# Gathering the expert rows by an order made with one-hot products, in a gated-attention and mixture-of-experts layer

## The chip, the cores and the metric

The kernel runs on one core of one Trainium2 chip. The metric is the device time of that core in microseconds (us), the median of several executions. Work is spread by hand over five engines: TensorE (PE; its weight loads are shown apart as PEld), VectorE (DVE), ScalarE (ACT), GpSimd (POOL) and SyncE (SP, which here only issues DMAs). Each has its own instruction stream, and they meet at semaphores. All data is fp32; one fp32 matmul stands in the trace as two passes, each with its own weight load.

## The reference, cut to what matters

The input is 2048 tokens (2 batches of 1024) of width 256.

```python
h = layernorm(x) * (1 + ca) + sa
x = x + ga * gated_linear_attention(h)          # 16 heads, chunks of 64
h = layernorm(x) * (1 + cb) + sb                # "h2" in the kernel
probs = softmax(h @ gate_w.T)                   # 8 experts
top_p, top_i = top_k(probs, 2)                  # two experts a token
y = sum over the two experts e of top_p * ((silu(h @ fc1[e].T) * (h @ fc2[e].T)) @ proj[e].T)   # 176 wide
shared = (silu(h @ sfc1.T) * (h @ sfc2.T)) @ sproj.T                                             # 704 wide
x = x + gb * (y + sigmoid(h @ shared_gate.T) * shared)
```

## The kernel before, in words

Tokens go in 4 blocks of 512 (`BLK`), 16 tiles of 128. Attention is a software pipeline over the blocks, `s` = 0 to 4. In its last round and after it stand the parts of the shared expert. A part is either `U` (block, f): two halves SA and SB of the up projection for 128 hidden channels, `silu_up` on ACT and `mult_up` on DVE, six of them a block, the last one half as large; or `D` (block, jj): the down projection of two token tiles, evicted on DVE by `add_down`. `SHARED_PARTS` lists them in order, and `FILL_PLACES` says how many stand at each named place between the steps of the routing. The parts take turns in two PSUM banks, `work[0]` and `work[1]`, so each matmul of a part waits until the part before the last has been evicted. Parts of the last block from `EARLY_UP` on come after the experts.

Routing: the top two experts of each token are found on DVE; `picked` (one-hot rows) times a triangular matrix on PE gives each token's rank within its expert; `routing_b` turns ranks into `pos`, the place of the token's two copies in an order sorted by expert, in which each expert starts on a multiple of 128. There are at most 39 tiles (`ETILES`) of one expert each.

The sorted rows then go through HBM. SP fills `xs_sorted` with zeros (10 DMAs) while attention ends. POOL scatters the 16 token tiles twice, 32 indirect DMAs (line 592), each row with 7 columns behind its 256 values (token number, weight, batch and so on). When all have landed, SP loads the sorted rows by pairs of tiles (line 457) into `xt`, four pairs of room. POOL works out from the extra columns of a loaded pair where its results go (`goals`, lines 604 to 613).

Experts: for each pair, PE does `rows_T` (transposes), `up` (line 1710), `hid_T` and `down` (lines 1731 to 1738); ACT and DVE stand between; DVE's `evac_y` writes the weighted result to `yout`, two pairs of room, and POOL scatters it to its token's row of `ys_tokens` by `put_rows` (39 indirect DMAs, line 621). The groups 1 to 3 of eight tiles are one hardware loop (`Fori`) on PE, ACT, DVE and SP; POOL's instructions are written out.

Tail: when all results have landed, SP loads them back (8 DMAs, line 474). PE meanwhile computes the rest of the shared expert of block 3 (`U` from `EARLY_UP` on, then two `D`), DVE adds everything (`combine`, lines 1330 to 1336, and `add_scaled_down`, line 1043), and SP stores the output.

Of the kernel before, what the change touches and what calls it, by code (L numbers as in the profile page):

```python
# [23 lines left out]
P = 128  # L24
# [26 lines left out]
XS_ROWS = ESLOTS * P  # L51
HX = HID + 7
NOWHERE = 1 << 20
X_TOK, X_W0, X_BATCH, X_TURN, X_DW, X_NONE, X_EXP = range(HID, HX)
# [10 lines left out]
def unit_order():  # L65
# [58 lines left out]
    fill(NBLK, "scatter")  # L124
    for f in range(EARLY_UP, FTS):
# [9 lines left out]
EARLY_UP = 4  # L135
SHARED_PARTS += [("U", NBLK - 1, f) for f in range(EARLY_UP)]
FILL_PLACES = [(4, "gates", 1), (4, "half", 1), (4, "second", 1), (4, "norm", 5), (4, "stats", 1), (4, "ln", 3),
               (4, "transposed", 2), (4, "top2", 1), (4, "scatter", len(SHARED_PARTS))]
FILL = {}
for slot_, place_, n_ in FILL_PLACES:  # L140
    FILL[slot_, place_] = SHARED_PARTS[:n_]
    del SHARED_PARTS[:n_]
UNITS = unit_order()
# [10 lines left out]
def adaln_moe(nc, x, cT, wmod, wq, wk, wv, wg1, wg2, bg2, wgate, norm_w, wo,  # L154
              router, e_up, e_down, s_up, s_down, out):
    with ExitStack() as ctx:
# [9 lines left out]
        xs_dram = nc.dram_tensor("xs_sorted", (XS_ROWS, HX), F32, kind="Internal").ap()  # L166
# [12 lines left out]
        h2tok = sb("h2tok", [P, NTILE, HX])  # L179
# [17 lines left out]
        def part(n):  # L197
# [28 lines left out]
        zero_row = state[:, :, :, :, :].rearrange("p a g v c -> p (a g v c)")[:, 0:HX]  # L226
# [24 lines left out]
        wq_sb, wk_sb, wv_sb, wgate_sb, wo_sb = (sb(n, [P, KC, HID]) for n in  # L251
                                                ("wq_sb", "wk_sb", "wv_sb", "wgate_sb", "wo_sb"))
# [17 lines left out]
        iota_i = sb("iota_i", [P, ESLOTS], I32)  # L270
        iota_f = sb("iota_f", [P, ESLOTS])
# [24 lines left out]
        pos_u = sb("pos_u", [P, TOPK, NTILE], U32)  # L296
        texp = sb("texp", [P, ESLOTS])
        texp_u = sb("texp_u", [P, ESLOTS], U32)
        texp1 = sb("texp1", [P, ESLOTS])
        tok_i = sb("tok_i", [P, NTILE], I32)  # L300
        second = sb("second", [P, XPAIRS, 2])
        turned = sb("turned", [P, XPAIRS, 2, 3])
        goal = sb("goal", [P, XPAIRS, 2, 3])
# [4 lines left out]
        yout = er_pos[:, :, :].rearrange("p a (t c) -> p a t c", t=2)  # L308
# [6 lines left out]
        xs_zero = sem("xs_zero")  # L315
# [23 lines left out]
        picked_ready, rank_full, rank_read, dlog_ready, pexp_ready, posu_ready, texp_ready = (  # L339
            sem(n) for n in ("picked_ready", "rank_full", "rank_read", "dlog_ready", "pexp_ready", "posu_ready",  # L340
                             "texp_ready"))
        xs_ready, ld_xt, xt_full, xT_ready, up_full, esilu_done, h_ready = (
            sem("xs_ready"), [sem(f"ld_xt{i}") for i in range(XPAIRS)], sem("xt_full"), sem("xT_ready"),
# [56 lines left out]
        def _(sp):  # L400
# [60 lines left out]
            for q in range(XPAIRS):  # L461
                load_pair(q, q)
# [6 lines left out]
            for j, s in enumerate(ys_stored):  # L469
                sp.wait_ge(s, 16 * len(range(j, ETILES, 4)))  # L470
# [1358 lines left out]
```

## Time and profile before

| what | value |
|---|---|
| median of 3 runs | 430.16 us (429.12 to 430.85) |
| the profiled execution, its own time | 429.87 us |
| its span, first to last instruction | 428.1 us |
| mean granted TensorE clock in the span | 0.970 of full |
| instructions in the span | 9797 |

The span is 1.77 us shorter than the time of the same execution; what a change saves in the span it saves in the time. Of the span, roughly the first 240 us are attention and routing, up to 306 us shared parts while rows are scattered, up to 403 us the experts, and then the tail.

### The profile page before, as it was taken

To read this page: it belongs to the slowest core of one execution; us is meant where nothing else is said; L and a number is where in the kernel's file an instruction comes from. 1 tells how busy PE (TensorE), PEld (TensorE's weight loads), DVE (VectorE), ACT (ScalarE), POOL (GpSimd) and SP (SyncE) were. 2 spreads that over 40 slices of the span, in tenths; PEclk is the share of its full clock that TensorE was granted. 3 is DMA by queue.
4 is the path that set the end of the run, shared out by engine and by line. 5 is a ranking of instruction groups with operands and counts; after the bars stand their busy time and mean duration, and the time that the engine had idled before them with its cause. 6 is when DMAs were issued, how large, how long until landed. Compare 5 with 4: busy or idle time off the path is not lost.

```text
span 428.1 us, 9797 instructions
## 1 busy us (share of the span) xinstructions
PE 380.2 (89%) x3833; PEld 231.2 (54%) x3834; DVE 235.4 (55%) x543; ACT 143.6 (34%) x296; POOL 146.8 (34%) x252
## 2 busy tenths in 40 slices
PE   3988889999899998999989999519999999999795
PEld 3345656474656566447545546304566666666353
DVE  3169656896698579214824811014265555656457
ACT  3567337535561503430324011001334333332010
POOL 8405006100610440020000377744047667676400
PEclk9999999999999999999999999858999999999789
DMA  8930300000000000499900023240133333321098
GB/s 272 295 109 7 98 4 2 2 3 4 2 3 3 2 2 5 148 308 287 254 12 2 26 101 114 101 152 12 33 96 109 101 98 110 107 69 47 33 315 273
DMA packets 32573, 39.83 MB, mean 93 GB/s; under 512 B 4231, under 2 KB 29202, under 8 KB 32532
## 3 DMA queue, kind: packets, MB, share of 16 engines
q1 hardware_dynamic: 29124, 30.74, 24.8%
q0 software_dynamic: 3408, 8.51, 5.6%
q8 instruction: 29, 0.48, 0.5%
q14 instruction: 12, 0.10, 0.1%
HBM read 23.24 MB, written 16.91 MB: 94 GB/s over the span
## 4 chain that ended last, share of the span: by engine, by line
PE 73%; DVE 10%; another core or an unknown queue 6%; ACT 5%; issue 3%; DMA 1%; SPq 0%; DVEq 0%; ACTq 0%
PE work L1361 17%; PE at_ps L1710 12%; PE work L1394 5%; PE work L1375 4%; PE work L1731 4%; PE at_ps L1430 4%; PE work L1733 3%; PE work L1522 3%; PE work L1572 2%; PE at_ps L1394 2%; PE at_ps L1694 2%; PE o_even L1485 2%; PE work L1354 2%; PE at_ps L1572 1%
## 5 line engine op out<-in xcount | busy, mean ns | idle before, releaser
L621 POOL DMA_INDIRECT ys_tokens<-er_pos,goal_u x39 | 40.6, 1041 | 43.3 <-DVE er_pos L1285 37.5
L1710 PE MATMUL at_ps<-arena 128*128 x156 | 54.5, 472 | 0.4 <-ACT arena L847 0.4
L592 POOL DMA_INDIRECT xs_sorted<-h2tok,pos_u x32 | 31.7, 989 | 66.1 <-DVE pos_u L955 56.6
L1375 PE MATMUL work<-sdn_sb,hs 128*128 128x256 f32 x192 | 48.6, 395 | 5.9 <-issue 5.9
L641 ACT ACTIVATE hs<-work 128x512 f32<-128x512 f32 (+1 forms) x24 | 14.3, 596 | 112.0 <-PE work L1361 93.9
L1027 DVE TENSOR_TENSOR hs<-work,hs 128x512 f32<-128x512 f32 (+1 forms) x24 | 16.6, 691 | 58.1 <-PE work L1361 44.3
L1375 PEld LDWEIGHTS work<-sdn_sb,hs 128*128 128x128 f32 x192 | 34.3, 190 | 19.1 <-issue 15.9
L554 POOL TENSOR_TENSOR sq<-sq,sg 128x512 f32<-128x512 f32 x8 | 10.0, 1274 | 99.9 <-issue 99.9
L1361 PE MATMUL work<-h2T,sup_sb 128*128 128x512 f32 x80 | 36.1, 597 | 1.1 <-DVE hs L1027 0.7
L1710 PEld LDWEIGHTS at_ps<-arena 128*128 128x128 f32 x156 | 26.5, 190 | 14.9 <-issue 6.6
L851 ACT ACTIVATE arena<-at_ps 128x176 f32<-128x176 f32 x39 | 12.4, 318 | 57.7 <-PE at_ps L1710 43.0
L1361 PE MATMUL work<-hT,sup_sb 128*128 128x512 f32 x40 | 22.9, 741 | 9.4 <-DVE tmp L1057 8.8
L1285 DVE SCALAR_TENSOR_TENSOR er_pos<-work,goal,sq 128x256 f32<-128x256 f32 x39 | 17.2, 480 | 21.4 <-PE work L1738 20.5
L1361 PEld LDWEIGHTS work<-h2T,sup_sb 128*128 128x128 f32 x80 | 14.8, 190 | 19.0 <-issue 15.4
L1265 DVE TENSOR_TENSOR arena<-at_ps,arena 128x176 f32<-128x176 f32 x39 | 13.3, 342 | 20.4 <-ACT arena L851 17.9
L1126 DVE COPY_PREDICATED arena<-causal,at_ps 128x512 f32<-128x512 uint32 x32 | 20.5, 718 | 5.9 <-PE at_ps L1430 5.9
L1057 DVE SCALAR_TENSOR_TENSOR tmp<-work,sgate,rows 128x256 f32<-128x256 f32 x12 | 5.2, 478 | 32.6 <-remote 25.2
L1361 PEld LDWEIGHTS work<-hT,sup_sb 128*128 128x128 f32 x40 | 9.5, 243 | 23.3 <-issue 11.7
L1430 PE MATMUL at_ps<-arena 32*64 32x128 f32 x512 | 17.8, 278 | 3.3 <-DVE gate_pair L1106 1.9
L1430 PEld LDWEIGHTS at_ps<-arena 32*64 32x64 f32 x512 | 14.1, 131 | 9.6 <-issue 9.0
L1361 PE MATMUL work<-za,sup_sb 128*128 128x512 f32 x40 | 17.4, 595 | 0.6 <-DVE tmp L1057 0.6
L1522 PE MATMUL work<-wv_sb,hT 128*128 128x256 f32 x64 | 15.8, 387 | 2.1 <-ACT sg L782 1.7
(243 smaller groups left out, 750.5 us busy)
## 6 DMA issues: line engine op xcount, KB each, us to landing
xs_sorted<-state SPq DMA_DIRECT2D x10, 526.0 KB, 11.4
h2tok<-xs_sorted SPq DMA_DIRECT2D x20, 263.0 KB
arena<-ys_tokens SPq DMA_DIRECT2D x8, 512.0 KB, 7.4
arena<-in_e_up SPq DMA_DIRECT2D x8, 352.0 KB, 5.5
x_sb<-in_x SPq DMA_DIRECT2D x4, 512.0 KB, 6.8
out_rows<-x_sb SPq DMA_DIRECT2D x16, 128.0 KB, 4.0
sup_sb<-in_s_up SPq DMA_DIRECT2D x2, 640.0 KB, 4.9
hs<-in_wmod SPq DMA_DIRECT2D x1, 1024.0 KB, 7.4
```

The lines of the kernel that those rows point to most:

```text
L592: g.indirect_dma_start(out=xs_dram, out_offset=bass.IndirectOffsetOnAxis(ap=pos_u[:, k, t:t + 1], axis=0), in_=h2tok[:, t, :], in_offset=N ...
L621: g.indirect_dma_start(out=ys_dram, out_offset=bass.IndirectOffsetOnAxis(ap=goal_u[:, i:i + 1], axis=0), in_=yout[:, q % 2, u, :], in_offs ...
L1027: v.tensor_tensor(hs[0:m, f, :], linear, hs[0:m, f, :], ALU.mult).then_inc(hs_ready, 1)
L1126: v.copy_predicated(atm[:, n % 2, j, :], causal[:, :, :].bitcast(U32).rearrange("p r l -> p (r l)"), at_ps[j][:, :]).then_inc(atm_ready, 1)
L1285: v.scalar_tensor_tensor(out=yout[:, (u // 2) % 2, u % 2, :], in0=work[u % 2][:, 0:HID], scalar=goal[:, (u // 2) % XPAIRS, u % 2, 1:2], in ...
L1361: ins = t_.matmul(o[0:m, :], sup_sb[:, k, w, f0:f0 + m], h2T_of[blk][:, k, :], start=(k == 0), stop=(k == KC - 1))
L1375: ins = t_.matmul(o[:, t * HID:(t + 1) * HID], hs[0:m, f, tk], sdn_sb[0:m, f, :], start=(f == 0), stop=(f == FTS - 1))
L1394: ins = t_.matmul(o[:, :], w[:, k, gr * P:(gr + 1) * P], rhs[:, k, :], start=(k == 0), stop=(k == KC - 1))
L1430: ins = t_.matmul(at_ps[j][CHUNK * e:CHUNK * (e + 1), q * P:(q + 1) * P], kh[r, gr, c * CHUNK:(c + 1) * CHUNK], qeo[r, gr, c, :, :].rearra ...
L1522: ins = t_.matmul(o[:, t * HID:(t + 1) * HID], hT[:, k, tk], wv_sb[:, k, :], start=(k == 0), stop=(k == KC - 1))
L1710: ins = t_.matmul(at_ps[2 + u % 2][:, 0:2 * FE], xT[:, u % 2, k * P:(k + 1) * P], eup[:, bass.ds(e, 1), k, :].rearrange("p a n -> p (a n)" ...
L1731: t_.matmul(work[t][:, 0:HID], hTe[:, w % 2, t * P:(t + 1) * P], main[:, bass.ds(e[t], 1), :].rearrange("p a n -> p (a n)"), start=True, s ...
```

## The change

The sorted rows no longer go through HBM.

- Each block's h2 rows are stored to HBM as they are, in token order (4 DMAs by SP, `store_h2`). The zero fill, the 7 extra columns, the 32 scatters, SP's pair loads and POOL's `goals` go.
- `routing_b` splits `pos` into tile and row within the tile (four small DVE operations in place of one cast). `tile_columns` (DVE, three operations on 128x640 for each of the two copies) makes for each token the one-hot row of its tile, times its token number plus one, and times its weight. `row_columns` (DVE, two on 128x1024 for each copy) makes the one-hot row of its row. 32 products of the second with the first on PE (128 tokens each, 80 columns, summed in `at_ps[3]`) give the table `rec`: for every row and tile of the sorted order, the token and the weight. `read_records` (DVE) makes gather and scatter indices of it.
- POOL fetches the rows of each expert tile by an indirect DMA (39 gathers, `gather_pair`), four pairs first, then two more, and from then on two gathers after each pair's two scatters.
- `yout` has room for four pairs instead of two and stands in another buffer. DVE's groups 1 to 3 are written out instead of looped.
- `EARLY_UP` is 0 instead of 4: `U` (3,0) to (3,3) move from before the experts to behind them. Of the nine parts from `D` (1,1) to `D` (2,1), five stand at the place "places", before the 32 products, and four at "gather", behind them. In the tail the first three `combine` stand between the `mult_up`.

The core of the diff:

```diff
-EARLY_UP = 4
+EARLY_UP = 0
-               (4, "transposed", 2), (4, "top2", 1), (4, "scatter", len(SHARED_PARTS))]
+               (4, "transposed", 2), (4, "top2", 1), (4, "places", 5), (4, "gather", 4)]
@@ SP
+            def store_h2(b):
+                sp.wait_ge(h2tok_ready, b + 1)
+                sp.dma_start(h2_dram[b * BLK:(b + 1) * BLK, :].rearrange("(t p) c -> p t c", p=P),
+                             h2tok[:, b * TPB:(b + 1) * TPB, :]).then_inc(h2_stored, 16)
...
-            for i in range(ESLOTS // 4):
-                sp.dma_start(xs_dram[i * BLK:(i + 1) * BLK, :].rearrange("(t p) c -> p t c", p=P),
-                             zero_row.unsqueeze(1).broadcast_to([P, TPB, HX])).then_inc(xs_zero, 16)
-            sp.wait_ge(xs_ready, 16 * TOPK * NTILE)
-            for q in range(XPAIRS):
-                load_pair(q, q)
...
+            store_h2(NBLK - 1)
@@ POOL
-            for k in range(TOPK):
-                for t in range(NTILE):
-                    g.indirect_dma_start(out=xs_dram, out_offset=bass.IndirectOffsetOnAxis(ap=pos_u[:, k, t:t + 1], axis=0),
-                                         in_=h2tok[:, t, :], in_offset=None).then_inc(xs_ready, 16)
...
+            def gather_pair(q):
+                slot = q % XPAIRS
+                for u in range(min(2, ETILES - 2 * q)):
+                    i = 2 * q + u
+                    if q >= XPAIRS:
+                        pool.wait_ge(xt_full, i - EGRP + 1)
+                    g.indirect_dma_start(out=xt[:, slot, u, :], out_offset=None, in_=h2_dram[:, :],
+                                         in_offset=bass.IndirectOffsetOnAxis(ap=token_u[:, i:i + 1], axis=0)
+                                         ).then_inc(ld_xt[slot], 16)
...
-            for q in range(EPAIRS):
-                if q + 2 < EPAIRS:
-                    goals(q + 2)
-                put_rows(q)
+            pool.wait_ge(token_ready, 1)
+            for q in range(XPAIRS):
+                gather_pair(q)
+            pool.wait_ge(goal_ready, 1)
+            ahead = XPAIRS + 2
+            for q in range(XPAIRS, ahead):
+                gather_pair(q)
+            for q in range(EPAIRS):
+                put_rows(q)
+                if q + ahead < EPAIRS:
+                    gather_pair(q + ahead)
@@ DVE
+        def tile_columns(dve, v, steps, k):
...
+            steps.did(v.tensor_tensor(weight, iota_f[:, 0:ESLOTS].unsqueeze(1).broadcast_to([P, NTILE, ESLOTS]),
+                                      spread(tile_f[:, k, :]), ALU.is_equal))
+            steps.sync()
+            steps.did(v.tensor_tensor(token, weight, spread(tok_f[:, k, :]), ALU.mult))
+            steps.sync()
+            v.tensor_tensor(weight, weight, spread(pw[:, :, k]), ALU.mult).then_inc(rec_made, 1)
+
+        def row_columns(dve, v, k):
+            for t in range(0, NTILE, RCHUNK):
+                if k == 0 and t == 0:
+                    dve.wait_ge(h2_stored, 16 * NBLK)
+                v.tensor_tensor(in_row[:, k, t:t + RCHUNK, :], iota_f[:, :].unsqueeze(1).broadcast_to([P, RCHUNK, P]),
+                                row_f[:, k, t:t + RCHUNK].unsqueeze(2).broadcast_to([P, RCHUNK, P]), ALU.is_equal
+                                ).then_inc(rec_made, 1)
...
+            for n, (kind, blk, i) in enumerate(parts):
+                if n < 2:
+                    tile_columns(dve, v, steps, n)
+                (mult_up if kind == "U" else add_down)(blk, i)
+                if 1 <= n <= TOPK:
+                    row_columns(dve, v, n - 1)
+            read_records(dve, v, steps)
+            fill(NBLK, "gather")
...
-            with dve.Fori(1, ESLOTS // EGRP - 1) as grp:
+            for grp in range(1, ESLOTS // EGRP - 1):
                 group(grp * EGRP, grp * XPAIRS)
...
+            sums = iter(range(NTILE // 2))
             for f in range(EARLY_UP, FTS):
                 mult_up(NBLK - 1, f)
+                if f >= FTS // 2:
+                    combine(next(sums))
@@ PE
-            fill(NBLK, "scatter")
+            fill(NBLK, "places")
+            for k in range(TOPK):
+                for t in range(NTILE):
+                    if t % RCHUNK == 0:
+                        pe.wait_ge(rec_made, TOPK + k * (NTILE // RCHUNK) + t // RCHUNK + 1)
+                    ins = t_.matmul(at_ps[3][:, 0:NREC * ESLOTS], in_row[:, k, t, :],
+                                    in_tile[k][:, t, :, :].rearrange("p a i -> p (a i)"),
+                                    start=(k == 0 and t == 0), stop=(k == TOPK - 1 and t == NTILE - 1))
+            ins.then_inc(rec_full, 1)
+            fill(NBLK, "gather")
...
             pe.wait_ge(shev_done, 2 * NBLK - 2)
             pe.wait_ge(mln_done, 2 * NBLK)
             pe.wait_ge(rank_read, 2)
+            pe.wait_ge(rec_ready, 1)
```

## Rows read from the trace of the kernel before

**Rows 1.** The page: busy time, share of the span and instructions of each engine.
```profile
PE 380.2 (89%) x3833; PEld 231.2 (54%) x3834; DVE 235.4 (55%) x543; ACT 143.6 (34%) x296; POOL 146.8 (34%) x252
```
**Rows 2.** Chain that ended last, in order of time: start us, us, what.
```profile
241.70 17.43 PE work L1361 x40
...
261.55 25.82 another core or an unknown queue
...
288.31 16.33 PE work L1361 x32
```
**Rows 3.** Windows: busy us and instructions of each engine, clock, DMA.
```profile
262.00:288.00 26.00, 11.60 (x43) 7.45 (x41) 0.82 (x3) 0.00 (x0) 16.20 (x18) 0.77 0.34 116
...
306.00:398.00 92.00, 90.98 (x432) 59.62 (x431) 52.49 (x132) 32.60 (x95) 57.35 (x120) 1.00 0.30 90
```
**Rows 4.** Timeline 240 to 290 us: start, us, engine, line, operation, idle before.
```profile
240.78 0.87 DVE L1057 SCALAR_TENSOR_TENSOR tmp<-work,sgate,rows 128x256 f32<-128x256 f32 x2
...
241.80 1.66 POOL L592 DMA_INDIRECT xs_sorted<-h2tok,pos_u  x1 [56.60 <-DVE pos_u L955]
...
267.73 3.58 PE L1375 MATMUL work<-sdn_sb,hs 128*128 128x256 f32 x14
...
278.92 0.58 PE L1375 MATMUL work<-sdn_sb,hs 64*128 64x256 f32 x1 [0.81 <-issue]
...
284.68 48.69 SPq L457 DMA_DIRECT2D h2tok<-xs_sorted  x11
...
287.39 0.87 DVE L1057 SCALAR_TENSOR_TENSOR tmp<-work,sgate,rows 128x256 f32<-128x256 f32 x2 [25.18 <-remote]
```
**Rows 5.** DMA queues, 260 to 262 us: packets, MB, share of 16 engines.
```profile
q8 instruction: 1, 0.02, 3.2%
```
**Rows 6.** The page's groups: count, busy us, mean ns of one, idle before.
```profile
L621 POOL DMA_INDIRECT ys_tokens<-er_pos,goal_u x39 | 40.6, 1041 | 43.3 <-DVE er_pos L1285 37.5
...
L592 POOL DMA_INDIRECT xs_sorted<-h2tok,pos_u x32 | 31.7, 989 | 66.1 <-DVE pos_u L955 56.6
...
L1027 DVE TENSOR_TENSOR hs<-work,hs 128x512 f32<-128x512 f32 (+1 forms) x24 | 16.6, 691 | 58.1 <-PE work L1361 44.3
```
**Rows 7.** Chain in order of time: two `D` parts of block 0.
```profile
190.32 11.73 PE work L1375 x48
```
**Rows 8.** Timeline, smaller DVE operations and the rank products on PE.
```profile
234.66 0.49 PE L1683 MATMUL at_ps<-yT,tri 128*128 128x128 f32 x2
...
234.99 0.39 PE L1684 MATMUL at_ps<-yT,ones 128*128 128x128 f32 x2
...
235.48 0.29 DVE L919 COPY yT<-at_ps 128x128 f32<-128x128 f32 x1 [1.65 <-PE at_ps L1684]
...
236.67 0.17 DVE L929 TENSOR_SCALAR ntl_i<-cnt_i 128x8 int32<-128x8 int32 x1
```
**Rows 9.** Timeline from the start of the experts.
```profile
304.49 0.60 PE L1694 MATMUL at_ps<-ident,h2tok 128*128 128x128 f32 x4
...
313.15 1.45 PE L1710 MATMUL at_ps<-arena 128*128 x4
...
314.61 1.10 POOL L621 DMA_INDIRECT ys_tokens<-er_pos,goal_u  x1 [20.00 <-DVE er_pos L1285]
...
316.01 1.03 POOL L621 DMA_INDIRECT ys_tokens<-er_pos,goal_u  x1 [0.30 <-issue]
...
317.98 1.45 PE L1710 MATMUL at_ps<-arena 128*128 x4
```
**Rows 10.** Timeline of the tail.
```profile
403.23 6.60 PE L1361 MATMUL work<-hT,sup_sb 128*128 128x512 f32 x8 [0.63 <-DVE er_pos L1285]
...
406.19 7.17 SPq L474 DMA_DIRECT2D arena<-ys_tokens  x8
...
411.38 11.89 PE L1375 MATMUL work<-sdn_sb,hs 128*128 128x256 f32 x48
...
424.94 0.88 DVE L1043 SCALAR_TENSOR_TENSOR x_sb<-work,sgate,x_sb 128x256 f32<-128x256 f32 x2
```

More of the change, by code:

```diff
@@ L50 @@
 XPAIRS = EGRP // 2
-XS_ROWS = ESLOTS * P
-HX = HID + 7
 NOWHERE = 1 << 20
-X_TOK, X_W0, X_BATCH, X_TURN, X_DW, X_NONE, X_EXP = range(HID, HX)
+NREC = 2
+RCHUNK = 8
 NROUT = NE + 1
@@ L142 @@
     del SHARED_PARTS[:n_]
+assert not SHARED_PARTS
 UNITS = unit_order()
@@ L295, in adaln_moe @@
         pos = sb("pos", [P, TOPK, NTILE])
-        pos_u = sb("pos_u", [P, TOPK, NTILE], U32)
+        tile_i = sb("tile_i", [P, TOPK, NTILE], I32)
+        tile_f = sb("tile_f", [P, TOPK, NTILE])
+        row_f = sb("row_f", [P, TOPK, NTILE])
+        tok_f = sb("tok_f", [P, TOPK, NTILE])
         texp = sb("texp", [P, ESLOTS])
         texp_u = sb("texp_u", [P, ESLOTS], U32)
[L299 to L303, printed above, removed]
+        tok_i = sb("tok_i", [P, TOPK, NTILE], I32)
+        rec = sb("rec", [P, NREC, ESLOTS])
+        token_u = sb("token_u", [P, ESLOTS], U32)
+        turn_at, token_1, token_0, in_batch1, empty, goal = (yflat[:, i * ESLOTS:(i + 1) * ESLOTS] for i in range(6))
         goal_u = sb("goal_u", [P, ESLOTS], U32)
         row_step, row_gain = sq[:, 0, 0:HID], sq[:, 1, :].rearrange("p (a n) -> p a n", a=2)
-        yout = er_pos[:, :, :].rearrange("p a (t c) -> p a t c", t=2)
+        yout = h2T[:, :, :, :].rearrange("p a k (t c) -> p (a k) t c", t=2)
         ld_x = [sem(f"ld_x{i}") for i in range(NBLK)]
@@ L841, in _ @@
             fill(NBLK, "top2")
-            fill(NBLK, "scatter")
+            fill(NBLK, "places")
+            fill(NBLK, "gather")
             def evac_rows(i, u):
@@ L902, in routing_a @@
                             ALU.subtract).then_inc(dlog_ready, 1)
-            steps.did(v.tensor_scalar(h2tok[:, :, X_EXP], topf[:, 1, :], 1.0, None, ALU.add))
             dve.wait_ge(pexp_ready, 1)
@@ L1259, in _ @@
             fill(NBLK, "top2")
-            fill(NBLK, "scatter")
+            parts = FILL[NBLK, "places"]
+            for n, (kind, blk, i) in enumerate(parts):
[5 more added lines that the diff above has]
+            read_records(dve, v, steps)
+            fill(NBLK, "gather")
             def expert_h(i, u):
@@ L1284, in evac_y @@
                 dve.wait_ge(gain_ready, i0 + u + 2 - u % 2)
[L1285 to L1286 removed]
+                v.scalar_tensor_tensor(out=yout[:, u // 2, u % 2, :], in0=work[u % 2][:, 0:HID],
+                                       scalar=rec[:, 1, i0 + u:i0 + u + 1], in1=row_gain[:, u % 2, :],
                                        op0=ALU.mult, op1=ALU.mult).then_inc(y_out, 1)
             def y_slot_free(i0, u):
[L1291 to L1293 removed]
+                if i0:
+                    dve.wait_ge(ys_stored[u], 16 * (i0 // EGRP))
             def group(i0, q0, tiles=EGRP, first=False):
@@ L1684, in _ @@
             t_.matmul(at_ps[2][:, P:2 * P], ones[:, :], pv, start=True, stop=True).then_inc(rank_full, 1)
-            fill(NBLK, "scatter")
+            fill(NBLK, "places")
+            for k in range(TOPK):
[6 more added lines that the diff above has]
+            ins.then_inc(rec_full, 1)
+            fill(NBLK, "gather")
             def rows_T(i, u):
                 if u % 2 == 0:
-                    pe.wait_ge(ld_xt[u // 2], 16 * (i // EGRP + 1) if isinstance(i, int) else i0_loads(i, u))
+                    pe.wait_ge(ld_xt[u // 2], (32 if i + 1 < ETILES else 16) + 32 * (i // EGRP) if isinstance(i, int) else i0_loads(i, u))
                 at_least(pe, xT_ready, i, -1)
```

135 lines of the change are left out of this document (62 added, 73 removed).

## The prediction

> **What bounds the kernel now.** I read four views in this order. The page's first part says who is busiest: PE, 89% of the span, with DVE and POOL far behind [rows 1]. So a gain has to come out of PE's stream or out of the 11% in which it stands. The chain that ended last says where it stands: it is PE nearly everywhere, except for one piece of 25.82 us from 261.55 on that belongs to no engine [rows 2]. The windows put a size on it: from 262 to 288 us PE is busy 11.6 of 26 us, DVE 0.8, ACT 0, POOL 16.2, and the granted clock is 0.77; in the experts, 306 to 398, PE is busy 90.98 of 92 us [rows 3].
>
> The timeline shows what kind of gap it is [rows 4]. DVE waits for the first `D` of block 2 until 287.39 ("remote", so no instruction of the record explains it), though the matmuls recorded for it were over by about 267. PE's last recorded passes are sparse, up to 278.92, and then it waits for DVE. All this time POOL issues scatters, from 241.80 on; SP begins to load sorted rows at 284.68, and DVE goes on 2.7 us later. So PE's signals do not come through while POOL issues scatter behind scatter, and come back when that is over. A fetch on an instruction queue lies at the beginning of it [rows 5]; whether it is the cause no row says.
>
> What did the gap cost? PE's work from 241.70 to the experts is 40+4 passes of `U` of block 2 (17.43 + 1.73 = 19.2 us), two `D` (11.73 for 48 passes) and `U` (3,0) to (3,3), 32 passes at 17.43/40 = 0.436 us, 13.9 us [rows 2, 7]. That ends at 241.7 + 19.2 + 11.7 + 13.9 = 286.5; the experts begin at 304.49 [rows 9]. So 18 us are lost. Part of them was due anyway only if PE had been without work: the rows were in SBUF at about 287, the time the parts fill.
>
> **The change, part by part.**
>
> *Routing.* Four dependent operations of 0.17 us, 0.2 with their wait, take the place of one cast, and a few small ones go: +0.6 us before `D` (1,0) is evicted [rows 8], and PE waits for that eviction.
>
> *Columns on DVE.* A 128x512 operation takes 0.69 us [rows 6], a 128x128 one 0.29 [rows 8]: 1.04 ns a column. So 128x640 takes 0.82 and three with their waits 2.6 us; 128x1024 takes 1.22, two 2.4. `tile_columns` (0) stands before the eviction of `D` (1,1), whose bank the second half of `U` (2,0) needs: PE has the first half's 1.7 us as cover plus nothing else, so it stands about 2.4 us. `tile_columns` (1) delays `mult_up` (2,0), and PE stands another 0.5. The two `row_columns` fall beside matmuls (3.5 us a part against 2.4 + 0.69 on DVE) and cost nothing; were they not covered, 5 us. I take +3.0; bounds 1 (only what exceeds the bank turns) and 8.
>
> *32 products on PE.* 64 passes. The rank products, four passes with 128 columns and a new weight load each, start at 234.66 and 234.99, two passes in 0.33 including the first load, and both pairs are over in 0.72 us [rows 8]; the four transposes take 0.60 [rows 9]. Taking off the drain of the last (0.3), a pass is 0.11 us, and 80 columns cannot be under half of that. 64 x 0.11 = +7 us. Bounds: 3.5, and 0.165 a pass by the 0.33 for two, 10.6.
>
> *What follows.* `U` (2,4), (2,5) and two `D` as before. The zero fill, scatters and pair loads go with the 18 us of the gap. The 4 stores of h2 are long done: they are issued while DMA is idle or, the last, at about 220 us, 30 before `row_columns` waits for it. New is that nothing of PE's stands between the eviction of `D` (2,1) and the first `rows_T`: two evictions 0.87 [rows 4], crossings, and the load of the expert numbers into registers, for which there is no row uncovered. I take 3 us, between 1.2 and 4. POOL's gathers begin about 1.4 us after the products (five small DVE operations) and eight of them take 8 x 1.3 = 10.4, while the parts behind them take 5.2 + 11.7 = 16.9: covered, with 4 us to spare after landing.
>
> Start of the experts: 241.7 + 0.6 + 3.0 + 19.2 + 7 + 11.7 + 3 = 286.2 instead of 304.49, **-18.3 us**.
>
> *Experts.* PE goes through a pair in 317.98 - 313.15 = 4.83 us without a pause [rows 9, 3], and nothing of its work changes. POOL's does: per pair two scatters as now, two gathers in place of `goals`. The second scatter starts 1.40 us after the first, both together last 2.43 [rows 9]; the mean of one is 1.04 [rows 6] plus 0.30 between. At 1.34 each, four take 5.36, 0.53 more than PE. The lag grows over the 13 pairs that still have a gather behind them to 6.5 us. The gather of pair q + 6 is issued behind the scatters of q and needed three of PE's pairs later. From the first scatter at 1.5 us after PE's turn of a pair, 2.7 + 2.7 for the four DMAs and 2.4 to land leave 15.9 - 9.3 = 6.6 us. So it just holds. `yout` with four pairs tolerates more than that. Price per indirect DMA: 0.99 + 0.30 at the low end (lag 4.3, hidden) and 1.66 + 0.30 at the high end, the one on DVE's busy moment at 241.80 [rows 4], which would be 7.8 us a pair, (7.84 - 4.83) x 13 - 6.6 = 33 us. The 39 scatters of this very stage are the nearer row; I take **+0.5 us**. The written-out groups on DVE cost nothing: DVE has 40 us to spare here [rows 3].
>
> The Trainium skill, page SBUF — State Buffer, section "SBUF: two separate sides", says that GpSimd can't write descriptors while DVE is in a two-port mode, as fp32 copies within SBUF are, and gives 3.1 us in place of 0.62. By it the sum would be far on the slow side if DVE's work here were such copies. The scatters' 1.04 against 0.99 beside a nearly idle DVE says that it isn't.
>
> *Tail.* Four `U` parts more on PE at full clock, 13.9 us: PE's stream bounds the new tail, while result loads (7.17 us of issue from 406.19 on) and `combine` fit beside it [rows 10]. The eight passes at half speed (6.60 us) are there before and after. Now PE ends at 411.38 + 11.89 = 423.27, and DVE, kept by `combine`, gets to the last eviction at 424.94; three `combine` go ahead in the new order, so this 1.4 us goes. **+12.5 us**.
>
> Sum: -18.3 + 0.5 + 12.5 = -5.3 us; span 428.1 - 5.3 = 422.8, time 424.6. The profiled execution (429.87) is 0.3 below the median of the runs, so I say **424.7 us**.
>
> **The rivals.**
>
> *The gap comes back (slower).* The mechanism is that of [rows 4]: PE's signals are held while POOL issues DMA behind DMA. POOL will do so in the eight gathers, and through two thirds of the experts with pauses under 1 us. For it: nothing in the trace shows a cause that the change removes, other than the density. Against: in the experts scatters run by twos and PE isn't held. In the gathers it would cost at most 6 us, since PE's stream went on for some 5 us of matmuls after the last signal. In the experts a held PE soon leaves POOL without work, so one hold is about lag plus landing, 5 to 8 us; from one hold on it is no faster, with two it is 424.7 + 12 = 437. The skill's Runtime: NRT & Kernel Launch, section "Instruction fetch mechanics", has each engine fetch 16 KiB blocks by a DMA queue of its own, and calls it mostly hidden; [rows 5] fit the size, and the cost is not hidden if this is the cause.
>
> *POOL bounds the experts (slower from 1.55 us on).* At c us per DMA the delay is (4c - 4.83) x 13 - 6.6: 2 us at 1.37, 8 us at 1.5, 13 at 1.6. It speaks for it that each DMA now has a wait of its own: the pair's spacing is 1.40, not 1.30. 427 to 438 us.
>
> *Larger gain.* The clock stays full in the tail (-3.3 us: eight passes at 0.436) or covers are better: 418 to 421.
>
> *The shift does nothing.* If the gap were due work of PE and not a hold, the experts would start 18 us later than I say, and the time would be 443. The sparse passes and the late signal speak against it.
>
> **How the numbers follow.** The forecast (421 to 428) 0.60, larger gain 0.12, gap back 0.13, POOL-bound beyond 2 us 0.12, nothing gained from the gap 0.03. The range 419 to 433 leaves out about 0.2. Within 0.5% (428.0 to 432.3), about what a measurement of this kernel can tell from no change: half of the POOL case and a third of the gap's, 0.12; faster 0.72, slower 0.16.
>
> **What would show it.** First `rows_T` at 284 to 288 us; no piece of the chain over 5 us without an engine; the products 6 to 8 us with a spacing of 0.11; pairs at 4.83 us throughout, and POOL's lag behind the evictions growing by about 0.5 us a pair to the fourteenth; PE at the end of the chain, its last `D` some 14 us later after the experts than now. Wrong would make it: a piece "unknown queue" inside the experts, `rows_T` waiting for a gather, or products at over 0.2 us a pass.

## The result and the profile after

| | before | changed |
|---|---|---|
| median of 4 runs each, us | 430.5 (429.12 to 435.44) | 446.76 (441.86 to 447.23) |
| ratio | | 1.033, 95% interval 1.022 to 1.044 |
| profiled execution, us (span) | 429.87 (428.1) | 447.23 (445.5) |

The changed kernel is slower by 3.3% (here and below ratios compare the means of executions within 1.5% of the fastest of their kernel, while medians and ranges have all of them). The forecast of 424.7 us and its range up to 433 both missed; what came true of the mechanisms is told below. The page of the changed kernel, first the engines as in [rows 1], then the two groups of POOL and the eviction whose rows POOL scatters, as in [rows 6]:

```profile
PE 393.0 (88%) x3897; PEld 241.6 (54%) x3898; DVE 246.0 (55%) x561; ACT 143.3 (32%) x296; POOL 127.1 (29%) x154
...
L589 POOL DMA_INDIRECT h2tok<-h_rows,token_u x39 | 38.5, 987 | 105.2 <-DVE token_u L978 84.7
...
L598 POOL DMA_INDIRECT ys_tokens<-h2T,goal_u x39 | 40.6, 1040 | 40.0 <-DVE h2T L1321 30.4
...
L1321 DVE SCALAR_TENSOR_TENSOR h2T<-work,rec,sq 128x256 f32<-128x256 f32 x39 | 17.1, 480 | 43.4 <-remote 25.6
```

PE is busy 12.8 us longer than before. The 64 passes of the products are 7.1 of it; moving parts adds nothing; another 3.9 is that the experts' 156 up passes take longer (L1757, 500 ns each against 472 before). The last row says what the forecast doesn't have: DVE waits 25.6 us in the experts' evictions for something that the trace doesn't explain ("remote").

The chain in order of time (start, length, what) shows the whole head and then where the time went:

```profile
248.73 13.98 PE work L1399 x28
262.71 7.10 PE at_ps L1728 x64
269.81 3.48 PE work L1399 x8
273.29 1.72 PE work L1392 x4
275.01 11.73 PE work L1413 x48
286.74 1.98 issue
288.71 0.42 PE at_ps L1741 x2
...
307.52 4.60 another core or an unknown queue
...
323.90 3.23 issue
...
339.16 4.68 another core or an unknown queue
...
358.31 4.53 issue
...
365.26 3.61 another core or an unknown queue
...
376.29 4.00 another core or an unknown queue
...
409.68 19.09 PE work L1399 x40
```

The piece of 25.82 us of [rows 2] is gone: from 248.73 to 286.74 PE runs from part to product to part, and then stands 1.98 us. But six pieces of 3 to 5 us in which no engine of the chain works, four of them called "unknown queue" as the old gap was, stand inside the experts. The windows (us, then busy us and instructions of PE, PEld, DVE, ACT, POOL, clock, DMA share, GB/s) set beside [rows 3]:

```profile
262.00:288.00 26.00, 24.74 (x126) 17.96 (x124) 6.39 (x18) 1.19 (x2) 7.83 (x8) 1.00 0.14 41
...
306.00:398.00 92.00, 77.82 (x340) 49.36 (x339) 41.37 (x105) 24.79 (x74) 55.90 (x55) 0.94 0.24 75
```

PE went from 11.60 to 24.74 busy us in the first window, and from 90.98 to 77.82 in the second. One hold from near, in the timeline (start, us, engine, line, operation, idle before):

```profile
309.82 0.97 POOL L589 DMA_INDIRECT h2tok<-h_rows,token_u  x1 [0.30 <-issue]
...
312.15 0.88 DVE L1321 SCALAR_TENSOR_TENSOR h2T<-work,rec,sq 128x256 f32<-128x256 f32 x2 [4.32 <-remote]
312.21 0.32 ACT L836 ACTIVATE arena<-at_ps 128x176 f32<-128x176 f32 x1 [3.91 <-PE at_ps L1757]
...
313.44 1.02 POOL L598 DMA_INDIRECT ys_tokens<-h2T,goal_u  x1 [2.65 <-DVE h2T L1321]
...
313.98 0.69 PE L1778 MATMUL work<-arena 128*128 x2 [1.84 <-DVE arena L1307]
```

DVE waits for down products whose last pass is recorded as over by 308.8, ACT for up products of a later tile. Both are let go within 0.06 us of each other, 1.4 us after the end of POOL's last gather before its pause (309.82 + 0.97 = 310.79). POOL had paused for want of an eviction. Then everything resumes and PE, at last, waits 1.84 us for DVE. I call this a hold. The list of waits in the experts (289 to 409 us: engine, line, waited for, total us, times, longest) adds them up, and the windows behind it show the stretches of half clock in the experts:

```profile
DVE h2T L1321 <- remote: 25.6, 6, 4.8
...
PE work L1778 <- DVE arena L1307: 13.2, 7, 3.3
...
PE work L1778 <- issue: 3.2, 1, 3.2
...
ACT arena L836 <- remote: 13.1, 4, 5.7
```
```profile
327.70:331.10 3.40, 3.40 (x10) 1.61 (x9) 0.49 (x3) 0.61 (x2) 1.90 (x2) 0.50 0.33 107
358.40:361.80 3.40, 3.40 (x10) 1.77 (x9) 1.28 (x4) 0.01 (x1) 2.51 (x3) 0.50 0.26 88
385.70:389.10 3.40, 3.40 (x9) 2.30 (x10) 1.22 (x3) 0.70 (x2) 1.00 (x1) 0.51 0.19 41
```

DVE's six long waits are not one for one the chain's six pieces: the one from 351.25 to 356.06 lies beside work of PE's in the chain, and the piece at 358.31 is a wait of ACT's. What PE itself loses in these rows is 13.2 + 3.2 = 16.4 us of standing before the down products, less 2.3 that it also stands at the last two tiles before the change, and 3 x 1.7 us for three stretches at the lower clock (1.2 GHz), which begin 0.3 to 1.8 us after PE went on from a stand: 14.1 + 5.1 = 19.2 us.

**The account, stage by stage.** Start of the rank products, start and end of the experts, and the tail up to the end of the span, all in us:

| | rank products | experts | their length | tail |
|---|---|---|---|---|
| before | 234.7 | 304.5 to 402.6 | 98.1 | 25.5 |
| changed | 236.9 | 288.7 to 409.0 | 120.3 | 36.5 |

From the rank products to the experts it is 51.8 instead of 69.8: -18.0. The rank products themselves start 2.2 later, a drift of the stages in front, which the change hardly touches (over the profiled executions of all variants below it lies between 233.6 and 243.2). Experts +22.2, tail +11.0. Together 17.4 = 445.5 - 428.1.

### The profile page after: what moved, and what is told of

It reads as the page before. It is cut to its first block, busy times and chain, and to the rows that moved or that the text cites. A ratio compares the mean times of both kernels' runs of the same rounds, so it can differ in the third digit from the quotient of the medians.

```text
span 445.5 us, 9617 instructions
## 1 busy us (share of the span) xinstructions
PE 393.0 (88%) x3897; PEld 241.6 (54%) x3898; DVE 246.0 (55%) x561; ACT 143.3 (32%) x296; POOL 127.1 (29%) x154
## 4 chain that ended last, share of the span: by engine, by line
PE 71%; DVE 10%; issue 7%; ACT 5%; another core or an unknown queue 4%; DMA 1%; DVEq 0%; SPq 0%; ACTq 0%
PE work L1399 15%; PE work L1413 9%; PE at_ps L1757 8%; PE work L1432 5%; PE at_ps L1468 4%; PE work L1778 3%; PE work L1560 3%; PE work L1610 2%; PE work L1780 2%; PE at_ps L1432 2%; PE o_even L1523 2%; PE at_ps L1728 2%; PE work L1392 2%; DMA hs<-in_wmod 1%
## 5 line engine op out<-in xcount | busy, mean ns | idle before, releaser
L589 POOL DMA_INDIRECT h2tok<-h_rows,token_u x39 | 38.5, 987 | 105.2 <-DVE token_u L978 84.7
L1757 PE MATMUL at_ps<-arena 128*128 x156 | 58.4, 500 | 0.4 <-ACT arena L832 0.4
L598 POOL DMA_INDIRECT ys_tokens<-h2T,goal_u x39 | 40.6, 1040 | 40.0 <-DVE h2T L1321 30.4
L1321 DVE SCALAR_TENSOR_TENSOR h2T<-work,rec,sq 128x256 f32<-128x256 f32 x39 | 17.1, 480 | 43.4 <-remote 25.6
L1757 PEld LDWEIGHTS at_ps<-arena 128*128 128x128 f32 x156 | 28.4, 203 | 16.7 <-issue 9.3
L1778 PE MATMUL work<-arena 128*128 x40 | 12.9, 405 | 16.4 <-DVE arena L1307 13.2
L1302 DVE TENSOR_TENSOR arena<-at_ps,arena 128x176 f32<-128x176 f32 x39 | 13.2, 339 | 20.1 <-ACT arena L836 14.6
L1399 PE MATMUL work<-za,sup_sb 128*128 128x512 f32 x40 | 19.6, 645 | 3.4 <-DVE tmp L1086 3.4
L1399 PE MATMUL work<-hT,sup_sb 128*128 128x512 f32 x40 | 19.1, 639 | 0.6 <-DVE h2T L1321 0.6
L832 ACT ACTIVATE arena<-at_ps 128x256 f32<-128x256 f32 x39 | 14.8, 383 | 14.3 <-PE at_ps L1741 13.6
L1741 PEld LDWEIGHTS at_ps<-ident,h2tok 128*128 128x128 f32 x78 | 11.2, 145 | 12.7 <-issue 9.0
```

What stands on the lines that cost most here:

```text
L589: g.indirect_dma_start(out=xt[:, slot, u, :], out_offset=None, in_=h2_dram[:, :], in_offset=bass.IndirectOffsetOnAxis(ap=token_u[:, i:i + ...
L598: g.indirect_dma_start(out=ys_dram, out_offset=bass.IndirectOffsetOnAxis(ap=goal_u[:, i:i + 1], axis=0), in_=yout[:, q % XPAIRS, u, :], in ...
L832: a.activation(xT[:, u % 2, :], at_ps[u % 2][:, 0:KC * P], ACT.Copy).then_inc(xT_ready, 1)
L1321: v.scalar_tensor_tensor(out=yout[:, u // 2, u % 2, :], in0=work[u % 2][:, 0:HID], scalar=rec[:, 1, i0 + u:i0 + u + 1], in1=row_gain[:, u ...
L1399: ins = t_.matmul(o[0:m, :], sup_sb[:, k, w, f0:f0 + m], h2T_of[blk][:, k, :], start=(k == 0), stop=(k == KC - 1))
L1757: ins = t_.matmul(at_ps[2 + u % 2][:, 0:2 * FE], xT[:, u % 2, k * P:(k + 1) * P], eup[:, bass.ds(e, 1), k, :].rearrange("p a n -> p (a n)" ...
```

## The experiments

The disputed term is +22.2 us in the experts against the forecast's +0.5. The theories: (a) POOL's dense indirect DMAs hold PE's signals, as in the old gap; (b) the bytes they move do it; (c) POOL is simply too slow and PE waits for rows. The 18 kernels ran in five groups, each group on one chip (0, 4, 1, 6 and 15) with its own runs of the kernel before beside it; which chip the first measurement ran on isn't known.

**First group: fewer POOL operations, or lighter ones.** e1 leaves out all gathers behind the first eight, e2 lets SP store the results, e3 is the kernel before with two pauses in the scatters, e4 cuts the later gathers to a quarter of their rows.

```diff
@@ e1: only the first eight gathers
-            for q in range(XPAIRS, ahead):
-                gather_pair(q)
             for q in range(EPAIRS):
                 put_rows(q)
-                if q + ahead < EPAIRS:
-                    gather_pair(q + ahead)
...
-                if u % 2 == 0:
+                if u % 2 == 0 and isinstance(i, int) and i < EGRP:
@@ e2: SP stores, POOL's scatter is taken out
+            for i in range(ETILES):
+                r = i % (TOPK * NTILE)
+                sp.wait_ge(y_out, i + 1)
+                sp.dma_start(ys_dram[r * P:(r + 1) * P, :], yout[:, (i // 2) % XPAIRS, i % 2, :]).then_inc(...)
@@ e3: before, pauses in the scatters
+                    if k * NTILE + t in (13, 26):
+                        pool.wait_ge(hs_ready, 3 * FTS if k * NTILE + t == 13 else 3 * FTS + 3)
@@ e4: short gathers
-                    g.indirect_dma_start(out=xt[:, slot, u, :], ...
+                    m = P if q < ahead else 32
+                    g.indirect_dma_start(out=xt[0:m, slot, u, :], out_offset=None, in_=h2_dram[:, :],
+                                         in_offset=bass.IndirectOffsetOnAxis(ap=token_u[0:m, i:i + 1], axis=0)
```

> The changed kernel without its last 31 gathers: only the first eight tiles are fetched, the later tiles are computed from whatever rows stand in the buffer, so the output is wrong in those. POOL then has two scatters a pair in the experts, as in the kernel before. Theory (PE's signals are held while POOL issues DMA behind DMA without a pause): no hold, pairs at 4.83 us, the experts about 98 us instead of 120, time about 425. Rival (the written-out groups on DVE, or the new buffers, slow the experts): the experts stay near 120 us and the time near 447. Rival (gathered rows arrive late): also about 425, but then the second experiment tells.

> The changed kernel with the 39 result scatters replaced by 39 plain stores of the same bytes from SyncE's queue, in the order of tiles (the results land in the wrong tokens' rows). POOL has the 39 gathers alone; bytes, landings and completions are the same. Theory (it is the density of POOL's own DMA stream): no hold, experts about 98 us, time about 425. Rival (the volume of transfers or of completions, whoever issues them): holds stay, 440 to 447.

> The kernel before, with two pauses in its stream of 32 scatters: after 13 of them POOL waits until DVE has finished the last up part of block 2, after 26 until it has finished U (3,2). Nothing is left out. Theory: the long hold from 262 to 287 us breaks up, PE works on, the experts begin at about 295 instead of 304 us, time about 421. Rival (the gap is due to something at that place, not to POOL's stream): the gap stays, and the scatters end later: 430 to 437.

> The changed kernel with the gathers from the seventh pair on cut to 32 of the 128 rows, so that each moves a quarter of the bytes; the other rows are stale, the output is wrong in them. Same number of DMAs and completions. Theory (density of POOL's stream): a gather on 32 rows may take POOL less time, then pauses appear and holds shrink, between 425 and 440; if it takes as long (0.95 us), the holds stay, about 446. Rival (bytes moved): holds gone even if POOL's time per gather is the same, about 425.

Measured: the kernel before itself took 416.51 us here (415.1 to 418.34, 7 runs), 14 less than in the measurement above. e1 took 425.3, e2 426.86, e4 421.98 (one run each), e3 424.86 (ratio 1.0215, 1.017 to 1.026). The experts took 99.7, 98.2, 99.7 and 99.7 us in e1, e2, e3, e4. No hold in any of them; but since the changed kernel did not run here, that said nothing yet about the theories. e3 was the first real blow: with pauses it should have won by the gap, to about 421, and it lost 2% against its own kernel before. In it PE waits 9.47 us for the late rows:

```profile
296.40 1.11 PE L1696 MATMUL at_ps<-ident,h2tok 128*128 128x128 f32 x4 [9.47 <-DMA h2tok<-xs_sorted]
```

So on this chip there was no gap for the pauses to remove, and the scatters had no time to give away. e4 also settled less than was hoped: a gather of 32 rows costs POOL 0.92 us in the mean, nearly as much as one of 128, so only the bytes are fewer in it.

**Second group: both kernels again, and the moved parts.** e7 is the changed kernel with the four `U` parts back in front of the experts; e8 the kernel before with one `combine` between each two `mult_up` of the tail.

```diff
@@ e7
-EARLY_UP = 0
+EARLY_UP = 4
...
-               (4, "transposed", 2), (4, "top2", 1), (4, "places", 5), (4, "gather", 4)]
+               (4, "transposed", 2), (4, "top2", 1), (4, "places", 5), (4, "gather", 8)]
@@ e8: before
+            sums = iter(range(NTILE // 2))
             for f in range(EARLY_UP, FTS):
                 mult_up(NBLK - 1, f)
+                if f < FTS - 1:
+                    combine(next(sums))
```

> The changed kernel as it is, beside the kernel before, to see whether the holds are there in this place and time: in the first four experiments no hold of PE's signals was to be seen, and the kernel before took 416.5 us instead of 430. If the holds depend on the chip or the hour and not on the code: no hold, about 423 to 425, against 416 to 417 of before (ratio 1.015 to 1.02). If POOL's density alone made them: they come back with the 39 full gathers, experts near 120 us, 440 to 447.

> The kernel before as it is, for its profile beside the others of this call. If before is at 416 us again: no gap from 262 to 287 us, PE ends the shared parts at about 286.5, and the experts begin at about 289 instead of 304.5, where the rows' arrival (about 287) sets it. If it is at 430: the gap is there.

> The changed kernel with EARLY_UP at 4 again: U (3,0) to (3,3) stand before the experts, at the place behind the products, as in the kernel before. PE's stream is the same, only in another order. By the sum of the prediction the experts begin 13.9 us later and the tail is 12.5 us shorter, so +1.4, minus up to 2 us because PE now has work while the last down part is evicted: the same as the changed kernel within 2 us. Rival (the eight gathers or the results' way back are the bound somewhere): faster by more than 4 us.

> The kernel before with one combine moved between the two mult_up of the tail, the one part of the change's tail that it can take. DVE comes to the last eviction 1.4 us late now; one combine taken out of its way (1.4 us) gives at most -1.4 us, 0.3%. If the first results have not landed when DVE asks for them, mult_up (3,5) and so PE's down parts wait: up to +2 us.

Measured: before 432.51 (429.39 to 437.98, 13 runs), e6 432.6, e5 444.11 (ratio 1.028, 1.020 to 1.036), e7 443.47 (1.025, 1.017 to 1.032), e8 432.34 (0.9995, 0.995 to 1.004). This chip is of the kind of the first measurement, and may be the same one. e6 has the gap and e5 has the holds. The chain of e6 and the window of e5's experts:

```profile
265.91 25.77 another core or an unknown queue
```
```profile
306.00:398.00 92.00, 80.27 (x354) 51.09 (x352) 43.04 (x108) 26.44 (x77) 57.49 (x57) 0.94 0.24 74
```

e7 starts its experts 14.2 us later than e5 (302.1 against 287.9), has a tail of 25.3 instead of 37.9, and experts of 115.4 instead of 117.8. So 14 us of parts cost the same on either side of the experts, and the holds are there either way. e8 changes nothing that this measurement can tell; the -1.4 us that were the most to expect lie inside its interval. It has the gap too: DVE waits 25.17 us in it.

**Third group: does the changed kernel have holds where before has no gap?** e9, e10 and e11 are e1, e2 and e3 again, e12 the changed kernel.

> The kernel of the first experiment (last 31 gathers left out, wrong rows in the later tiles) again, since the holds were absent from all kernels of the first call and present in all of the second. Beside a before of 430 to 433 (a chip with holds): theory of POOL's density says no hold, experts about 98 us, 425 to 428, that is below before; if PE's signals are held whatever POOL does, 440. Beside a before of 416: 425 again, no news.

> The kernel of the second experiment (scatters replaced by SyncE's plain stores, results in wrong rows) again. On a chip with holds: if the cause is POOL's own stream of indirect DMAs, no hold, about 427; if it is the volume of transfers and completions whoever issues them, holds stay, 436 to 447. On a chip without: 427 again.

> The kernel before with two pauses in its scatters, again. On a chip with holds: the hold lasts as long as POOL's stream does, so the first pause ends it or it does not begin before the last six scatters; the experts begin at about 296 instead of 304, and the time is 420 to 425 against 430 to 433. If the gap does not depend on pauses: 436 or more. On a chip without holds: 425 against 416.5, as in the third experiment.

> The changed kernel as it is, so that each call has it. On a chip with holds 442 to 447, as measured twice. On a chip without holds nothing has been measured: there its experts should take 98 us, and the time is 423 to 426 against 416.5 of before, ratio 1.015 to 1.023, since before has no gap to win there and the change adds about 10 us of PE's stream.

Measured: before 418.05 (414.15 to 422.82, 7 runs); e9 427.23, e10 424.04, e11 425.01 (1.018, 1.010 to 1.027), e12 428.69 (427.67 to 430.99; ratio 1.027, 1.021 to 1.033). I call such a chip quiet. e12 is the changed kernel, unedited, 18 us faster than in the first measurement, and still slower than before. Its experts, in the windows:

```profile
306.00:390.00 84.00, 82.98 (x395) 54.00 (x394) 48.67 (x123) 28.51 (x83) 62.98 (x62) 1.00 0.29 91
```

POOL is busy 75% of this stretch (61% above, where holds also stop POOL), DMA moves 91 GB/s (75 above), and PE is busy 98.8%. The density alone doesn't make holds, then, and neither do the bytes. The experts take 99.7 us in e12, as in e9 and e10 (99.7 and 99.6), so taking POOL's work away gives nothing there, and the groups of DVE that are written out cost nothing (99.75 in the kernel before, e15 below). Theory (c) is answered by the lists of waits of e12 and of the first measurement: in neither does PE wait for a DMA in the experts.

**Fourth group: what the kernel before does without its gap.** e13 is e3 and e14 is e4 again, e15 the kernel before with a profile, e16 the changed kernel with SP's stores and, in place of POOL's scatter, a second gather into rows that nobody reads:

```diff
-                    g.indirect_dma_start(out=ys_dram, ...
+                    if i >= 4:
+                        pool.wait_ge(spare_in[i % 4], 16 * (i // 4))
+                    g.indirect_dma_start(out=spare[:, i % 4, :], out_offset=None, in_=h2_dram[:, :],
+                                         in_offset=bass.IndirectOffsetOnAxis(ap=token_u[:, i:i + 1], axis=0)
+                                         ).then_inc(spare_in[i % 4], 16)
```

> The kernel before with two pauses in its 32 scatters, for the case that this chip has holds (before at 430 to 433). Theory (a hold begins in a long unbroken stream of POOL's indirect DMAs and ends with the stream): the gap of 25 us breaks up, experts from about 296 us, 420 to 425. If pauses do not matter: 436. On a chip without holds 425 for the third time.

> The changed kernel with the late gathers cut to 32 rows, again. On a chip with holds: if the number of POOL's DMAs in the stream makes them, the experts stay at 115 us or more, 440; if the bytes do, about 100 us, 423. On a chip without: 422 again.

> The kernel before, for its profile on this chip. At 430 to 433 it shows the gap once more. At 416 to 418 its PE stands nowhere for more than 3 us between 262 and 290, and the experts begin at 288 to 291 us instead of 304.5; the missing 14 to 16 us are then the whole difference between the two kinds of chip.

> The changed kernel with SyncE's plain stores in place of the scatters, and in the place of each scatter a second gather of the same rows into a spare buffer (results in wrong rows). POOL's stream is as dense as in the changed kernel, but nothing that it issues writes to HBM. On a chip with holds: if the density of POOL's stream makes them, experts at 115 to 120 us, 440 to 447; if the scatters' writes to HBM have to be in it, no hold, about 427. On a chip without: about 427.

Measured: before 416.61 us (414.36 to 545.47, 7 runs; the next highest is 419.66); e13 422.85 (1.016, 1.007 to 1.025), e14 431.91, e15 413.92, e16 427.08. No holds in any. e14 missed its 422 and e4, the same kernel, by 10 us. Its experts take 99.7 us like e4's; 8.5 of the 9.9 us between the two spans lie before the rank products (242.1 against 233.6), in stages that the edit doesn't touch, with a granted clock of 0.96 to 0.97 up to 180 us against 1.00 in e4. So single runs on two chips can lie 10 us apart while a stage in them agrees to 0.1 us. What this group is worth is e15, which shows the stretch of [rows 3] and [rows 4] undisturbed, with the same instructions: the window, then DVE at its first `D` of block 2, then the end of the chain before the experts.

```profile
262.00:288.00 26.00, 23.85 (x73) 12.86 (x73) 8.05 (x13) 2.39 (x4) 16.86 (x17) 1.00 0.33 110
```
```profile
265.76 0.87 DVE L1057 SCALAR_TENSOR_TENSOR tmp<-work,sgate,rows 128x256 f32<-128x256 f32 x2 [4.45 <-PE work L1375]
```
```profile
282.38 2.49 DMA xs_sorted<-h2tok,pos_u
284.89 2.83 DMA h2tok<-xs_sorted
287.77 0.45 PE at_ps L1694 x2
```

POOL scatters as densely as in [rows 3] (16.86 us against 16.20), and DVE gets its signal at 265.76 where it got it at 287.39. The experts begin at 287.8, bound by the last scatter and the loads behind it, with PE's parts just over: PE waits 2.15 us for them. The fetch of [rows 5] is here too, in the DMA queues at 260 to 262 us, and holds nothing:

```profile
q8 instruction: 1, 0.02, 2.9%
```

In the three profiles with the gap, though, such a fetch does lie within 0.3 us of the start of the chain's piece (before 261.3 and 261.55, e6 266.0 and 265.91, e8 262.6 and 262.61). In the changed kernel, between 288 and 409 us, this queue has three fetches, at 297.4, 320.3 and 396.7 us, and the other instruction queue, q14, two, at 345.2 and 387.9. Only the one at 320.3 lies in one of DVE's six waits. The Trainium skill, page Runtime: NRT & Kernel Launch, section "Instruction fetch mechanics", calls the cost of such a fetch mostly hidden; e15 agrees, with a fetch and no stand.

**Fifth group: the separation of (a) and (b), once more.** e17 is e2 and e18 is e4.

> The changed kernel with its 39 indirect stores of the experts issued by SP as plain stores of 128 rows to fixed places, so that the output's rows are not at their tokens; POOL then issues only the 39 gathers in the experts. If the holds come from POOL issuing without pause, they are gone wherever this runs: on a chip on which the kernel before takes about 430 us, the experts take 98 to 100 us and the kernel 424 to 428, against 444 of the changed kernel. If the holds come from the bytes moved or are a property of the chip whatever POOL does, the experts take 115 to 120 us and the kernel 440 to 446 on such a chip. On a chip on which the kernel before takes about 416 us both give 424 to 427, and the run tells nothing new.

> The changed kernel with its gathers from pair 6 on fetching only 32 of the 128 rows, so that most token rows of the experts are stale: POOL issues as many indirect operations as in the changed kernel, and the gathers move a quarter of the bytes. On a chip on which the kernel before takes about 430 us: if the holds come from POOL's dense issue, they stay, with experts of 112 to 120 us and 438 to 446 us in all; if they come from the bytes of the gathers, they go, with experts of 98 to 100 us and 422 to 430 us. On a chip on which the kernel before takes about 416 us both give 420 to 432.

Measured: before 416.63 (414.33 to 419.66, 7 runs); e17 425.94 (422.64 to 429.1; ratio 1.018, 1.008 to 1.028), e18 429.96 (422.1 to 453.29; ratio 1.018, 1.007 to 1.029). Again a chip of the quiet kind, and neither kernel has a hold; PE is busy 70.00 of 70 us from 310 to 380 in e18. Inconclusive on what it was made for.

## Why the prediction was wrong

**Right, within a microsecond or so.** From the rank products to the experts the forecast has 286.2 - 234.7 = 51.5 us, measured 51.8. Its parts: the 64 passes of the products take 7.10 us in the chain above, 0.11 each (+7). The columns make PE stand twice, 1.37 and 1.98 us, together 3.35, of which 0.6 stood before too (+3.0; the forecast had split it as 2.4 and 0.5, so that its sum came out is partly luck):

```profile
244.76 1.98 PE L1399 MATMUL work<-za,sup_sb 128*128 128x512 f32 x4 [1.37 <-DVE tmp L1086]
...
248.73 4.54 PE L1399 MATMUL work<-za,sup_sb 128*128 128x512 f32 x6 [1.98 <-DVE tmp L1086]
```

The stand with nothing of PE's in front of `rows_T` was taken as 3 and is 1.98. The gathers were taken at 1.3 apart and come at 1.25:

```profile
273.39 0.95 POOL L589 DMA_INDIRECT h2tok<-h_rows,token_u  x1 [0.30 <-issue]
274.64 0.95 POOL L589 DMA_INDIRECT h2tok<-h_rows,token_u  x1 [0.30 <-issue]
```

The tail was taken as +12.5 and is +11.0: the forty passes of `U` take 19.09 us instead of 13.9 + 6.6, because the lower clock lasts 3.4 us there (409.6 to 413.0) and lasted 6.8 before (402.3 to 409.1). POOL's mean in the experts, 61.43 us for 61 operations (a window of 306 to 409 us), plus 0.30 between is 1.31, taken as 1.34; on quiet chips the lag is hidden as forecast (experts of 99.7 us in e12). Its 6.6 us of slack came from 15.9 us where three pairs are 14.5; no `rows_T` waits for a gather, so nothing hung on it. The case of the Trainium skill, page SBUF — State Buffer, section "SBUF: two separate sides", in which DVE's copies hold such a DMA up, isn't met here: a gather took 0.99 us and a scatter 1.04 in the mean, with DVE busy 48 us beside them.

**The step that failed: the experts' term, +0.5 us, measured +22.2.** It rests on "PE goes through a pair in 4.83 us without a pause" and "nothing of its work changes". The only cost that the sum has there is POOL's lag; a hold inside the experts stood at nothing in it. Against the other terms the miss is small: the stretch before the experts is -18.0 (forecast -18.3), the tail +11.0 (+12.5), and the stages in front drifted by +2.2. That the late signals are what the experts lost is shown by e12: the same kernel, without holds, has experts of 99.7 us where they take 120.3 here.

**Behind it stands "So 18 us are lost", taken as a property of the old code that the change removes.** The 18 us were a hold, as the forecast read them, and they did go. But whether there are holds goes by the chip too, not by the code alone: four of five groups ran where no kernel had any. There the old scatters cost next to nothing, since 13.9 us of `U` parts and two `D` lie over them (e15: rows and PE ready together at 287.8), so the change has little to win. From the rank products to the experts it takes 51.8 us (e12) against 54.0 (e15), the experts 99.7 against 99.75, the tail 36.5 against 24.7: -2.2 and +11.8 are +9.6, and 10.6 were measured (428.69 - 418.05). The forecast's own terms without the 18 us (-13.9 + 0.6 + 3.0 + 7 + 3 before the experts, then 0.5 and 12.5) give +12.7, the 443 us of its last rival. On a quiet chip, what the change adds to PE's stream is paid nearly in full.

**And where holds exist, they moved.** The rival "the gap comes back" named the mechanism and the place, and had 0.13. Its price for one hold, 5 to 8 us, was too high: 22.2 us over six is 3.7 each. Its count, one or two, was too low. It argued from the gathers in front of the experts, and from "in the experts scatters run by twos and PE isn't held". The first was right: eight gathers, 10 us of POOL, and no hold. The second was evidence for the other side: before, POOL paused after every two; after, it issues four or more in a row for two thirds of the experts, and three of DVE's six waits end 1.4 to 1.5 us after POOL runs dry (at 312.15, 343.92 and 368.94 us), one 0.5 us after it (356.06) and two within 0.2 us of it (323.55 and 380.37). Behind the last gather, at 384.28 us, scatters run by twos, and no wait of that kind is left; ACT's longest there, 3.14 us, lies in the stretch of lower clock. The chance was the other mistake: it was given only 0.13, although, as the forecast says itself, no row offered a cause that the change took away.

**What stays open.** What makes a hold where there are any. An instruction fetch is not enough (e15), and five of the six waits in the changed kernel have none in them; whether one starts the old gap, where it lies at the beginning each time, is not shown. That POOL's indirect DMAs have part in it is argued from where they lie in six traces (before, changed, e5 to e8), not shown by an edit. In the old gap the release comes 4.5 us after the end of the last scatter:

```profile
281.94 0.96 POOL L592 DMA_INDIRECT xs_sorted<-h2tok,pos_u  x1 [0.30 <-issue]
```

In e6 and e8 it is 4.5 again, but the whole stretch repeats there with the same lengths (DVE waits 25.18, 25.13 and 25.17 us), so the three say no more than one: the end may as well hang on something else in the stretch. Each edit that thins the stream out or changes what it moves (e1, e2, e4, e16, and e3 on the old code) came to run only on quiet chips. Nor can I say whether it is the issue or the packets. That it is the chip at all rests on each group staying of one kind through all its runs; the groups also ran at different times, and something that changes with the hour, or other work on the same chip, is a rival that nothing here separates. The only edits that ran where holds are, e7 and e8, left them.

No version here beats the kernel before beyond the noise. The variants without POOL's scatters or without most gathers leave work out and are still 6 to 10 us slower than it on the same chip (e1, e2, e9, e10, e17).

## What to carry to other kernels

A stretch in which no engine works is only yours to win if you can say what makes it; one that the profile calls an unknown queue may come and go with the chip, so time the kernel on several before a change is built on it. Where one engine fills the span, add up first what the change puts on it and takes off it: here +7 of products and +5 of stands, against scatters that on a quiet chip had been hidden but for 2 us. If such a hold goes from one stretch, look for the next one in which the same engines work as densely, and count how often it can come, not only what one costs.

## What the runs showed of the hardware

The same kernel has medians of 416.5 to 418.1 us on four chips and of 430.5 and 432.5 in the first measurement and on a fifth, over 4 to 13 runs each. The difference lies in one stretch: from the rank products to the experts it takes 69.8 us with the hold and 54.0 without. For the changed kernel it is 428.69 against 444.11 and 446.76. In a hold PE's matmuls are recorded as over, and DVE and ACT go on late and sometimes within 0.1 us of each other; the longest waits in the experts are 4.8 us (DVE) and 5.7 (ACT), in the old gap 25.18. Where there are holds, one lies in the stretch of 32 scatters and none in that of eight gathers; on the quiet chips neither has one. An indirect DMA of 128 rows of 1 KB keeps POOL busy 0.95 to 1.04 us, with 0.30 to the next; one of 32 rows 0.92.
